# Gated recurrence on one core: pair 1 of layer 0 turned by TensorE, only pair 0 gathered in two parts

## The reference

```python
for i in range(6):
    gate = ih[i][token]
    state = jnp.tanh(state + jnp.matmul(state, hh[i]) * gate)
```

## Time and profile before

| what | us |
|---|---|
| median of 3 runs | 96.92 (96.0 to 97.68) |
| the profiled execution, device time | 97.14 |
| its span, first to last instruction | 95.3 |
| PE busy | 85.3 (89%) |
| DVE busy | 79.6 (83%) |
| ACT busy | 76.8 (81%) |
| POOL busy | 68.4 (72%) |

### The profile page before, as it was taken

One profiled execution on the slowest core, in us unless ns is written; L12 is line 12 of the kernel. 1 busy time (PEld: TensorE's weight loads), 2 busy tenths in 40 slices (PEclk: granted clock), 3 DMA queues, 4 the chain that ended last, 5 costly groups with the idle time before them and its releaser, 6 DMA issues.

```text
span 95.3 us, 1876 instructions
## 1 busy us (share of the span) xinstructions
PE 85.3 (89%) x688; PEld 76.1 (80%) x688; DVE 79.6 (83%) x128; ACT 76.8 (81%) x133; POOL 68.4 (72%) x63
## 2 busy tenths in 40 slices
PE   5957997999994988999999999999999999999900
PEld 5947885989873866998999999998999999988800
DVE  1239993969729799899998999989999999989980
ACT  5039999999974669998999989999899969975551
POOL 3487877877787089859988689877698589877000
PEclk9999999999999999999999999999999999999995
DMA  2899999852994905952545815556255515556984
GB/s 29 254 377 399 322 281 320 239 169 73 125 122 131 130 21 111 105 110 46 98 76 109 102 33 98 104 110 65 52 110 110 110 23 104 99 110 145 385 300 160
DMA packets 27224, 13.99 MB, mean 147 GB/s; under 512 B 23756, under 2 KB 24012, under 8 KB 27216
## 3 DMA queue, kind: packets, MB, share of 16 engines
q1 hardware_dynamic: 24720, 11.81, 56.1%
q0 software_dynamic: 2496, 2.07, 7.5%
HBM read 17.05 MB, written 2.10 MB: 201 GB/s over the span
## 4 chain that ended last, share of the span: by engine, by line
PE 51%; DVE 20%; DMA 15%; issue 6%; POOL 4%; ACT 0%; SPq 0%; POOLq 0%; DVEq 0%
PE products L298 43%; PE turned L330 7%; DVE gates L433 6%; DMA gates<-in_gate_rows,index 6%; DVE sums L471 5%; DMA last_rows<-in_gate_last 5%; POOL gates L275 4%; DVE sums L483 4%; DMA split_cols<-split_rows 4%; DVE split_rows L495 2%; DVE sums L468 1%; PE spare L339 1%; DVE split_cols L488 1%; ACT state L406 0%; PE spare L348 0%
## 5 line engine op out<-in xcount | busy, mean ns | idle before, releaser
L298 PE MATMUL products<-w_head,split_cols 128*128 128x256 f16 x316 | 55.0, 273 | 0.3 <-DMA split_cols<-split_rows 0.3
L282 POOL TENSOR_TENSOR sums<-sums,state 128x512 f32<-128x512 f32 x36 | 45.5, 1272 | 10.9 <-DVE sums L471 10.6
L298 PE MATMUL products<-w_rest,split_cols 128*128 128x256 f16 x158 | 43.1, 273 | 0.0
L406 ACT ACTIVATE state<-sums 128x512 f32<-128x512 f32 (+1 forms) x49 | 30.3, 619 | 10.7 <-DVE sums L483 5.1
L298 PEld LDWEIGHTS products<-w_head,split_cols 128*128 128x128 f16 x316 | 30.9, 98 | 4.0 <-DMA split_cols<-split_rows 0.6
L471 DVE SCALAR_TENSOR_TENSOR sums<-products,w_down,gates 128x512 f32<-128x512 f32 (+1 forms) x40 | 29.5, 737 | 2.2 <-PE products L298 2.2
L298 PEld LDWEIGHTS products<-w_rest,split_cols 128*128 128x128 f16 x158 | 15.5, 98 | 1.8
L290 PE MATMUL products<-w_full,first_cols 128*128 128x256 f32 x64 | 15.1, 381 | 1.6 <-DMA w_full<-in_weights 1.6
L275 POOL DMA_INDIRECT gates<-in_gate_rows,index x12 | 13.3, 1110 | 3.7 <-issue 3.4
L290 PEld LDWEIGHTS products<-w_full,first_cols 128*128 128x128 f32 x64 | 11.6, 190 | 3.0 <-issue 1.7
L370 ACT ACTIVATE gates<-last_rows 128x1536 f32<-128x1536 f32 (+1 forms) x8 | 10.6, 1390 | 4.2 <-DMA last_rows<-in_gate_last 4.2
(11 more groups left out here) (37 smaller groups left out, 46.9 us busy)
## 6 DMA issues: line engine op xcount, KB each, us to landing
first_cols<-in_state_cols SPq DMA_DIRECT2D x8, 256.0 KB, 4.5
out<-state SPq DMA_DIRECT2D x7, 256.0 KB, 2.4
w_full<-in_weights SPq DMA_DIRECT2D x6, 256.0 KB, 5.2
last_rows<-in_gate_last SPq DMA_DIRECT2D x1, 768.0 KB, 5.0
split_cols<-split_rows SPq DMA_TRANSPOSE x20, 3.1
out<-state SPq DMA_DIRECT2D x2, 128.0 KB, 1.7
gates<-in_gate_rows,index POOLq DMA_INDIRECT x12, 4.8
gates<-in_gate_first,index POOLq DMA_INDIRECT x4, 5.6
```

The lines of the kernel that those rows point to most:

```text
L282: nc.gpsimd.tensor_tensor(sums[:, q], sums[:, q], pair_rows(state, q), ALU.add).then_inc(pool_added, 1)
L298: last = nc.tensor.matmul(bank[:, j, :], split_cols[:, q, s, j, k, :], w[:, l - 1, k * HID:(k + 1) * HID], start=(n == 0), stop=(n == len( ...
L406: nc.scalar.activation(pair_rows(state, q)[:, cut], sums[:, q, cut], ACT.Tanh).then_inc(state_ready, 1)
```

## The change

Pair 1 of layer 0 goes by PE and not by DMA; in the other layers it still goes by DMA. In layer 0 the rests of the pairs that go by PE stand four steps after the pair's own step on DVE, and not five. FIRST keeps the tiles of pair 0 only. Tiles 2 and 3 are filled first, whole, and gathered whole, ahead of the others; the fills of the other tiles move accordingly (tile 15's is on DVE after step 1; the short fill after step 2 on DVE is gone). POOL issues 2 gathers of the first kind, 14 whole ones and 2 of the later layers, where it issued 4, 12 and 4.

```diff
-    PE_INSTEAD = ()
+    PE_INSTEAD = ((0, 1),)
...
+    FIRST_REST_LAG = 4
...
-    FIRST = (0, 1, 2, 3)
-    GATHERS = (4, 5, 6, 7, 8, 9, 10, 11, 12, 13, 14, 15, 0, 1, 2, 3)
-    ACT_FILLS = {-1: (5, 7, 10, 12, 14, 0, 1), 1: (2,)}
-    DVE_FILLS = {-1: (4, 6, 8, 9, 11, 13), 0: (15,), 2: (3,)}
+    FIRST = (0, 1)
+    GATHERS = (2, 3, 4, 5, 6, 7, 8, 9, 10, 11, 12, 13, 14, 15, 0, 1)
+    ACT_FILLS = {-1: (3, 5, 7, 10, 12, 14, 0), 1: (1,)}
+    DVE_FILLS = {-1: (2, 4, 6, 8, 9, 11), 0: (13,), 1: (15,)}
...
-                    if n == 0 and i >= REST_LAG and by_pe(i - REST_LAG):
+                    if n == 0 and FIRST_REST_LAG <= i < PAIRS + FIRST_REST_LAG and by_pe(i - FIRST_REST_LAG):
+                        make_rest(i - FIRST_REST_LAG)
+                    if n == 0 and i >= PAIRS + REST_LAG and by_pe(i - REST_LAG):
                         make_rest(i - REST_LAG)
```

## The result

The changed kernel took 97.96 us (median of 20 runs, 97.23 to 100.88), the kernel before 96.70 us (20 runs, 95.81 to 99.02). The ratio is 1.0136, with a 95% interval of 1.0109 to 1.0163: slower, by 1.4%, within the two per cent that were called no change. (Ratios here are those of the undisturbed runs, so they need not be the quotient of the medians.) The profiled execution of the changed kernel took 97.25 us, its span was 95.5 us: it was the second fastest of its 20. The profiled execution of before, 97.14 us, was among the slower half of its kind. Put beside each other these two say +0.1 us, as forecast, and the medians say +1.3. So the first thing to learn is what differs between two executions of one kernel.

What follows compares the result with a forecast made beforehand. The kernel was taken as bound by when PE can start step 13's product, 38.10 us; gains and added waits nearly cancelled to +0.1 us, giving 97.2 for the profiled execution and 97.0 for the median, range 95.8 to 98.4.

Steps and rivals of the forecast that it cites:

- second rival: Fourteenth gather still lands after 5.6 us even without pair 1's transpose: about 99.3 us; chance 0.10.
- first case: Whole kernel: no real change, within 0.6 us of the 97.0 us median; chance 0.58.
- The stage: PE runs gapless from step 13's product at 38.10 us; only what moves that start changes the time.
- fourth rival: PE's steps 14 on gain too, by more than 1.9 us; chance 0.02.
- own sign of being wrong: PE's gapless stretch begins more than 0.6 us away from 38.1, or is not gapless.
- Places on POOL: Gathers of tiles 5, 9, 13 and 15 stay sixth, tenth, fourteenth and sixteenth in POOL's row.
- times on POOL: Third gather starts at 7.45, then 1.44 + 0.30 each beside fills; tenth 18.2, fourteenth 23.6.
- first rival: Gathers cannot run beside DVE's copies, so the third waits for all six fills: +4.5 us, 101.5; chance 0.03.
- The wait for the bank: Pair 2's turn on PE waits for pair 0's rest until 23.2, some 0.8 us; totals follow at 31.5.
- The last step: Pair 5's transpose, issued at 34.4 behind two rests, takes 3.71 us; step 13's product starts 0 to 0.1 later.
- The gain of the removed transpose: Without pair 1's transpose, tiles 13 and 15 land in 3.0 us each, bounds 2.9 and 5.6.
- The third: No wait on the bank and pair 5's transpose lands sooner: 0.6 to 1.0 us faster; chance 0.27.

Runs made afterwards that it cites:

- e1: The changed kernel unaltered, run again against the kernel before: ratio 1.0123, profiled execution 98.05 us.
- e11: Second run of the kernel before with pair 1's turn by PE and all layer-0 rests four steps late, gathers and fills of before: ratio 1.0060, median 97.39 us.
- e8: The changed kernel with tile 0's short fill put first among ACT's fills: ratio 1.0146 against the kernel before.
- e10: The changed kernel without DVE's fills of tiles 4, 6, 8, 9 and 11, pairs 2 to 7 multiplied by pair 1's gates: ratio 1.0051 against the kernel before.
- e5: The kernel before unaltered, run again for its profile: ratio 1.0017, median 96.43 us over 12 runs.
- e9: As e6, but pair 1's turn gets a bank of its own, copies1: ratio 0.9924 against the kernel before, median 95.98 us.
- e3: The changed kernel's gathers and fills only, pair 1 by DMA and rests five steps late as before: ratio 1.0124 against the kernel before.
- e7: The changed kernel with only the rests of pairs 0 and 1 a step sooner: ratio 1.0153 against the kernel before.
- e6: The kernel before with pair 1's turn by PE and only the rests of pairs 0 and 1 a step sooner: ratio 1.0026.
- e12: Second run of e6, on one chip with e11: ratio 0.9978 against the kernel before, median 96.57 us.
- e4: The kernel before with only pair 1's turn by PE, rests five steps late, gathers and fills as before: ratio 1.0411.

## Why the prediction was right, and where it was not

The verdict was right: within two per cent, and the median of 97.96 lies in the range. The sum was wrong: +0.1 us was forecast, +1.3 measured. The right verdict owes something to luck: the range was wide for the spread of the runs and for a part of the second rival, and what filled it was neither. The median is 1.0 us above the 97.0 that was forecast for it, which is outside the first case (0.58) and is what was called slower by a mechanism of its own (0.13). And the profile of the changed kernel shows nearly the forecast numbers (fourteenth gather at 23.60, step 8's multiplication at 32.68, step 13's product at 37.94) only because its last row landed 0.45 us sooner than in the profile of before.

**The stage.** That all is decided by when PE's gapless stretch begins was right: in after it goes on from 40.14 with 2.62 and 0.44 by turns, as before, and the 0.1 by which it begins later than the earlier trace rows (40.14 against 40.02) is the 0.1 of the profiled times. So the fourth rival, a gain from step 14 on, is out. The prediction's own sign of being wrong was a stretch that begins more than 0.6 away from 38.1 or has a gap. Step 13's product at 37.94 and, in e1, 38.55 is within it, but behind it PE has a gap of 0.2 in after and 0.4 in e1, so by that sign the prediction was wrong there.

**Places on POOL** were right, **times on POOL** were the step that failed first. "With 0.30 of issue the third gather starts at 7.45": in e1, with the landing of before, it was 8.00. "From there they follow at 1.44 + 0.30": the third took 1.91. Together 1.0 us at the fourth gather (10.22, forecast 9.19), still 0.9 at the tenth (19.09, forecast 18.2). The row I took the 1.44 from was that of a gather that ran beside one and a half copies, and I read it as the price of any gather beside fills. The Trainium skill (SBUF — State Buffer, section SBUF: two separate sides) has the two take turns exclusively. The traces now agree, for one copy at a time: a gather that meets a copy ends 0.85 to 0.87 after the copy's end. My remark that a gather of 1.44 us speaks against it was wrong: such a gather had stood still in between. What the traces don't show is that POOL waits for the whole row of copies, since it goes on between two of them. The first rival, to which I gave 0.03, was this mechanism with too high a price: 4.5 us in place of about 1, because it let the third gather wait for all six.

**The wait for the bank** was right in kind: in e1 PE waited 0.63 ahead of pair 2's turn, for pair 0's rest. It began at 24.29, forecast 23.2, later by what the gathers were late. From there the sum of 8.3 us to the totals held (24.29 + 8.3 = 32.6; PE's totals are at 32.58); step 8's multiplication came 0.87 behind them (33.45), where I had taken 0.98; and 1.94 to the issue of pair 5's transpose held.

**The last step failed too.** "With 3.71 us the transpose lands at 38.1 to 38.2": it took 3.1 us in e1, the lower bound of that term, and the product started at 38.55. So of the 1.1 us by which the totals were late only 0.4 were left. But the next turn then waited for the state of step 10, which I had not followed: on ACT it stands behind the state of step 9, this hangs on POOL's addition of step 9, this on DVE's multiplication of step 9, and between step 8's and step 9's multiplication there stand now two rests. The rows of e1 above show it: POOL's addition at 36.13 (behind 0.58 us of idle time), ACT, PE's turn at 40.24, 0.4 later than the product's end. I priced pair 4's rest only by what it did to the transpose right behind it, 0.6. That was enough in e11, where PE waits for this transpose and for no state. It was not enough where the transpose lands early, in after, e1 and e8. The 0.4 at the product and the 0.4 behind it make the 0.8 by which e1 (98.05) lies above the forecast of 97.2.

**The gain of the removed transpose** (tile 13's gates 1.4 us sooner, in spite of a later gather) was mostly not there to be had. It was true of the profiled execution: without the transpose, the fourteenth landed in 3.3 to 3.9 us (4.2 in e10). In e5 it lands in time anyway. This, the base, is the other 0.4 us of the 1.2 by which I was off: the profiled execution of 97.14 lies that much above the median of before, 96.7. At equal landings the changed kernel is 0.9 longer than the profile of before (e1) and 1.2 longer than e5. One reading of the rows was off without moving the sum: ahead of the totals PE lost 1.58 us to the late addition, and not 2.

**The rivals.** The second (a late landing without the transpose) is out: 3.9 in e1. The third (faster) is out for the changed kernel. Half of its condition came true, pair 5's transpose landed after 3.1 to 3.2 us, and was used up by the late gathers. The other half, no wait on the bank, holds in e9, which is 0.8% faster than before.

The parts, then: gathers behind fills 1.2% (e3; e7 against e6), of which the slowed gathers are the larger share as far as e10 can tell; rests of pairs 2, 4 and 6 a step sooner 0.6 to 0.8% by themselves, hidden when the gathers are late; the turn nothing (e6, e12), with a loss at the bank that e9 puts at 0.5%. Their sum is more than the whole, 1.3%.

## What to carry to other kernels

A profile is one execution: when a chain rests on the meeting of two transfers half a microsecond apart, take a second profile of the same kernel before building on it. An instruction moved ahead has to be priced at everything that stands behind it on its engine, also two instructions on and by way of another engine. When a piece of work is put behind an event that scatters, here the landing of a load, the scatter comes with it. When a ring of buffers gets one more user, look for a buffer that is idle in just these steps before paying the wait or moving others to shorten it.

## What was not expected of the hardware

- A gather on POOL that waited for a fill began 0.81 to 0.83 us after the fill's end, in six profiles, with or without copies behind it on DVE, while one behind another gather begins 0.30 after it and the first, which waits for DVE's index, 0.29 after that.
- POOL's whole gathers took 1.91 and 1.44 us beside unbroken fp32 copies on DVE and 0.99 to 1.00 without. One that began during a single copy ended 0.85 to 0.87 after the copy's end, and the same holds of DVE's instruction for the first weight's rest (w_rest, e3: 24.50 and 1.39 us against an end at 25.02). DVE's rests of the state, which read PSUM, did nothing of the kind.
- After idle times of 2.43 us (e7) and 2.80 us (e4) PE was granted 0.52 and 0.50 of its clock in the next stretch of 2.4 to 2.9 us; after 2.07 us in e8 and 2.33 in e3 it kept 1.00. So a wait of PE can cost more than itself: 1.03 us on one product in e4.
